# Two graph attention layers on one Trainium2 core: the first step of the pipeline in a new order

## The reference, cut to what matters

```python
# layer 0
Q, K, V = x @ W_q + b_q, x @ W_k + b_k, x @ W_v + b_v        # 8 heads of 64
a, c = x @ w_g[:D], x @ w_g[D:]                                # gates of rows and columns
scores = QK^T / 8 + a[:, :, None] + c[:, None, :] + b_g + log(adj + 1e-9)
x1 = softmax(scores) @ V + x
# layer 1
scores = where(adj == 0, -1e18, (x1 @ Wq + bq) @ (x1 @ Wk + bk)^T / sqrt(512))
x2 = x1 + (softmax(scores), 0 where adj == 0) @ x1 @ Wc
out = layernorm(x2) * gamma + beta
```

## Time and profile before

| what | value |
|---|---|
| median of 3 runs | 2256.19 us (2255.06 to 2257.74) |
| the profiled execution: its own time | 2256.57 us |
| its span in the profile | 2254.7 us |
| PE busy | 2238.5 us, 99% of the span |
| DVE, ACT, POOL busy | 1794.6, 1223.6, 987.0 us |
| TensorE clock granted, mean | 0.997 of full |

### The profile page before, as it was taken

How to read it: one execution, slowest core, us unless ns; L and a number is a source line. 1 busy time by engine, 2 the same in 40 slices (tenths; PEclk the granted TensorE clock), 3 DMA queues, 4 the chain that set the end, 5 groups by cost and what they waited for, 6 DMA issues and landing times.

```text
span 2254.7 us, 39435 instructions
## 1 busy us (share of the span) xinstructions
PE 2238.5 (99%) x13258; PEld 1866.8 (83%) x13258; DVE 1794.6 (80%) x5363; ACT 1223.6 (54%) x3489; POOL 987.0 (44%) x1139
## 2 busy tenths in 40 slices
PE   9999999999999999999999999999999999999998
PEld 6788888888888888888888888888888888888886
DVE  6778788778788787887787887878887878878775
ACT  5555555555455555555554565555555545655553
POOL 0244354553445543545434455435454344554343
PEclk9999999999999999999999999999999999999999
DMA  7333333433344333333333433333343334333321
GB/s 244 113 123 117 118 126 127 131 109 127 112 137 127 123 116 123 122 126 129 106 131 110 139 127 122 117 117 128 120 132 109 131 110 139 127 119 121 117 94 57
DMA packets 189659, 277.46 MB, mean 123 GB/s; under 512 B 24593, under 2 KB 126097, under 8 KB 185233
## 3 DMA queue, kind: packets, MB, share of 16 engines
q1 hardware_dynamic: 189168, 274.42, 37.0%
q10 hardware_dynamic: 288, 0.52, 0.1%
HBM read 166.28 MB, written 108.59 MB: 122 GB/s over the span
## 4 chain that ended last, share of the span: by engine, by line
PE 94%; DMA 2%; DVE 2%; SPq 1%; ACT 0%; issue 0%; POOL 0%; DVEq 0%; POOLq 0%
PE bank L256 27%; PE bank L258 26%; PE bank L257 26%; PE bank L509 5%; PE bank L522 5%; PE bank L551 5%; DMA turn_dram<-turned 1%; DMA probsT<-turn_dram 1%; DVE x1n L1255 0%; DVE turned L1185 0%; DMA ident<-in_ident_in 0%; SPq L318 0%; ACT probs L863 0%; SPq L349 0%; DVE probs L1166 0%
## 5 line engine op out<-in xcount | busy, mean ns | idle before, releaser
L1547 POOL TENSOR_TENSOR probs<-probs,rcp 128x512 f32<-128x512 f32 x256 | 290.5, 1151 | 875.0 <-DVE rcp L1176 874.8
L863 ACT ACTIVATE probs<-probs,nmax 128x128 f32<-128x128 f32 x1024 | 397.5, 390 | 159.7 <-DVE nmax L1166 158.3
L1255 DVE STREAM_TRANSPOSE x1n<-x1T 32x512 f32<-32x512 f32 x496 | 348.6, 703 | 38.3 <-DMA out<-x1n 30.8
L1555 POOL TENSOR_TENSOR x_lo<-xT_land,x_hi 128x512 fp32r<-128x512 f32 x124 | 168.9, 1392 | 328.0 <-ACT x_hi L809 328.0
L847 ACT ACTIVATE k_sb<-bank,cols 128x512 f32<-128x512 f32 x128 | 88.2, 689 | 270.8 <-PE bank L551 168.0
L1166 DVE CUSTOM_DVE_ANT_0 probs<-bank,bias 128x128 f32<-128x128 f32 x1024 | 227.2, 286 | 2.8
L256 PE MATMUL bank<-wc_hi,x_hi 128*128 128x512 f32 x512 | 204.3, 399 | 0.0
L256 PE MATMUL bank<-wv_hi,x_hi 128*128 128x512 f32 x512 | 203.2, 397 | 0.6 <-ACT q_sb L852 0.6
L256 PE MATMUL bank<-x_hi,wq_hi 128*128 128x512 f32 x512 | 201.9, 394 | 0.0
L256 PE MATMUL bank<-x_hi,wk_hi 128*128 128x512 f32 x512 | 199.9, 391 | 0.2
L1192 DVE SCALAR_TENSOR_TENSOR x1T<-bank,cols,xT_land 128x512 f32<-128x512 f32 x124 | 93.0, 750 | 134.2 <-PE bank L522 126.8
(11 more groups left out here) (171 smaller groups left out, 5287.3 us busy)
## 6 DMA issues: line engine op xcount, KB each, us to landing
turn_dram<-turned SPq DMA_DIRECT2D x128, 512.0 KB, 2.6
probsT<-turn_dram SPq DMA_DIRECT2D x512, 128.0 KB, 2.7
xn<-in_x SPq DMA_DIRECT2D x126, 256.0 KB, 3.2
xT_land<-in_xT SPq DMA_DIRECT2D x31, 1024.0 KB, 7.4
out<-x1n SPq DMA_DIRECT2D x124, 256.0 KB, 2.0
adj_sb<-in_adj SPq DMA_DIRECT2D x32, 256.0 KB, 3.2
c_rows<-c_dram SPq DMA_DIRECT2D x32, 256.0 KB, 3.2
at_dram<-scratch SPq DMA_DIRECT2D x30, 256.0 KB, 2.0
```

Of the source, the lines that this page charges most:

```text
L863: op = nc.scalar.activation(probs[:, k, :], probs[:, k, :], ACT.Exp, bias=nmax[:, k:k + 1], scale=-1.0, accum_out=sums[:, k:k + 1])
L1255: op = nc.vector.transpose(x1n[b * BLK:(b + 1) * BLK, :, :] .rearrange("p g (c a s) -> p a c g s", c=C, a=P // BLK)[:, a, :, :, :], x1T[a ...
L1547: nc.gpsimd.tensor_tensor(probs[:, half, :], probs[:, half, :], rcp[:, half].unsqueeze(2).to_broadcast([P, HALF, P]), ALU.mult)\
L1555: nc.gpsimd.tensor_tensor(x_lo[:, c, :], xT_land[(t + 1) % 2][:, c, :], x_hi[:, c, :].bitcast(f32), ALU.subtract).then_inc(s["pool_x"], 1)
```

## The change

Only step 0 and its neighbourhood are edited; the order of steps 1 to 31 stays as it is.

- **Gate rows.** For step 0 the trip of c through DRAM is gone. DVE multiplies the identity by c's four columns (four 128x128 products into `c_rows`), and PE multiplies a matrix of ones with it into bank 3 (`spread_first_c`, one fp32 matmul of 512 columns, between scores 1 and v of graph 2). `bias(0)` reads bank 3.
- **Loads.** The identity and the four row blocks of x are issued ahead of the column chunks 2 and 3 of Wk and Wq. Wk lands in `x1T` and no longer in `v_sb`. `gamma_b` is loaded late, with `beta_b`, behind the c spread of step 1, since `col_sum` now lies in it; `row_sum` lies in `c_rows`.
- **M.** Chunks 0 and 1 stay where they were; k and q of pairs 2 and 3 come next, then the row term and the columns; chunks 2 and 3 go behind scores 3, the last of the step.
- **DVE.** The low parts of columns 2 and 3 go behind the gates. The row sum goes behind `maxima(0, 0)`, the column sum behind `turn(0, 1)`, gates 0 and 1 of step 1 behind the low part of Wc, gates 2 and 3 of step 1 to the end of the step.
- **ACT** follows: the high parts of columns 2 and 3 behind v 1, those of M's chunks 2 and 3 behind the exponentials of pair 2.
- **SP.** Pairs 0 and 1 of step 0 are moved ahead of the loads of x's rows 2 and 3 for step 1; the c spread of step 1 goes behind the move of pair 2.

The diff by its changed lines; new semaphores' waits that only rename (`s_beta` to `s_gb`, `v_sb` to `wk_land`) are cut.

```diff
-row_sum, col_sum = (probsT[1][:, 2 * i:2 * i + 2, :, :].rearrange("p a k s -> p (a k s)") for i in (0, 1))
+row_sum, col_sum = c_rows[:, :], gamma_b[:, :]
+wk_land = x1T
...
+s_diag = sem("dve_c_diagonal")
+s_spread = sem("pe_c_spread")
...
-        if t == 0 and c == 1:
-            sp.wait_ge(s_m, C + 2)
...
-        sp.wait_ge(s_cst0, 16 * (t + 1))
-        if t > 0:
-            sp.wait_ge(s["dve_b"], nth("dve_b", t - 1))
+        sp.wait_ge(s_cst0, 16 * t)
+        if t == 1:
+            sp.wait_ge(s_m, 3)
+        sp.wait_ge(s["dve_b"], nth("dve_b", t - 1))
...
-    load_columns(v_sb, wk, "k", 0)
+    load_columns(wk_land, wk, "k", 0)
...
-    load_columns(v_sb, wk, "k", 1)
+    load_columns(wk_land, wk, "k", 1)
...
-    for c in range(2, C):
-        load_columns(v_sb, wk, "k", c)
-        load_columns(xT_land[1], wq, "q", c)
...
+    sp.dma_start(ident[:, :], ident_in).then_inc(s_const, 16)
...
-    sp.dma_start(ident[:, :], ident_in).then_inc(s_const, 16)
...
+    for c in range(2, C):
+        load_columns(wk_land, wk, "k", c)
+        load_columns(xT_land[1], wq, "q", c)
...
-    sp.dma_start(gamma_b[:, :], gamma.to_broadcast([P, D])).then_inc(s_rows, 16)
...
         else:
-            spread_c(0)
+            sp.wait_ge(s_lo["k"], C)
...
+        if not it.l1:
+            move_probs(t, 0)
+            move_probs(t, 1)
...
-        move_probs(t, 0)
-        move_probs(t, 1)
-        if it.l1:
+            move_probs(t, 0)
+            move_probs(t, 1)
...
-        spread_c(t + 1)
+            spread_c(t + 1)
...
         if not it.l1:
-            sp.wait_ge(s_m, C + 1)
-            sp.dma_start(beta_b[:, :], beta.to_broadcast([P, D])).then_inc(s_beta, 16)
+            spread_c(t + 1)
+            sp.wait_ge(s_m, 4)
+            sp.dma_start(gamma_b[:, :], gamma.to_broadcast([P, D])).then_inc(s_gb, 16)
+            sp.wait_ge(s_m, C + 2)
+            sp.dma_start(beta_b[:, :], beta.to_broadcast([P, D])).then_inc(s_gb, 16)
...
-        elif d >= 2:
-            pe.wait_ge(s["act_v"], nth("act_v", 0, d))
+        elif d == 1:
+            pe.wait_ge(s["dve_b"], nth("dve_b", 0))
+        elif d == 2:
+            pe.wait_ge(s["act_k"], nth("act_k", 0, 3))
+        else:
+            pe.wait_ge(s["act_q"], nth("act_q", 0, 3))
...
+    def spread_first_c():
+        pe.wait_ge(s_diag, 1)
+        pe.wait_ge(s["act_q"], nth("act_q", 0, 1))
+        nc.tensor.matmul(bank[3][:, :], one_c.to_broadcast([P, P]), c_rows[:, :],
+                         start=True, stop=True).then_inc(s_spread, 1)
...
         else:
-            pe.wait_ge(s["act_k"], nth("act_k", 0, 3))
+            pe.wait_ge(s_lo["m"], 3)
...
         else:
-            pe.wait_ge(s["act_q"], nth("act_q", 0, 3))
+            pe.wait_ge(s_lo["m"], 4)
...
+        spread_first_c()
...
-        for d in range(C):
-            m_chunk(d)
+        m_chunk(0)
+        m_chunk(1)
+        pe.wait_ge(s_lo["m"], 1)
+        project_k(0, 2)
+        pe.wait_ge(s_lo["m"], 2)
+        project_q(0, 2)
+        pe.wait_ge(s["act_v"], nth("act_v", 0, 2))
+        project_k(0, 3)
+        pe.wait_ge(s["act_v"], nth("act_v", 0, 3))
+        project_q(0, 3)
...
-        for c in range(2, 4):
-            pe.wait_ge(s_lo["m"], 2 * c - 3)
-            project_k(0, c)
-            pe.wait_ge(s_lo["m"], 2 * c - 2)
-            project_q(0, c)
...
+        m_chunk(2)
+        m_chunk(3)
...
     def m_high(d):
-        act.wait_ge(s_m, d + 1)
+        act.wait_ge(s_m, d + 1 if d < 2 else d + 3)
...
+        q_out(0, 1)
+        log_adj(0, 1, 0)
+        v_out(0, 0)
+        v_out(0, 1)
...
-        q_out(0, 1)
-        log_adj(0, 1, 0)
-        act.wait_ge(s_lo["k"], C)
-        v_out(0, 0)
-        v_out(0, 1)
...
-        v_out(0, 3)
...
+        v_out(0, 3)
...
-        m_high(2)
...
-        m_high(3)
...
-        for c in range(2, 4):
-            exps(0, c, 0)
-            exps(0, c, 1)
+        exps(0, 2, 0)
+        exps(0, 2, 1)
+        m_high(2)
+        m_high(3)
+        exps(0, 3, 0)
+        exps(0, 3, 1)
...
-    for c in range(2, C):
-        wk_low(c)
-        wq_low(c)
...
-        dve.wait_ge(s_crow, 16 * (t + 1))
+        if t == 0:
+            dve.wait_ge(s_spread, 1)
+            c_row = bank[3][:, :].rearrange("p (g j) -> p g j", g=GG)
+        else:
+            dve.wait_ge(s_crow, 16 * t)
+            c_row = c_rows[:, :].rearrange("p (j g) -> p g j", g=GG)
...
-        c_row = c_rows[:, :].rearrange("p (j g) -> p g j", g=GG)
...
-            dve.wait_ge(s_cst0, 16 * t)
+            if t > 1:
+                dve.wait_ge(s_cst0, 16 * (t - 1))
...
-    dve.wait_ge(s_const1, 16 * 2)
-    dve.wait_ge(s_wld1["q1"], 16 * C)
-    dve.wait_ge(s_wld1["k1"], 16)
+    dve.wait_ge(s["dve_a"], nth("dve_a", 0, 3))
+    for g in range(GG):
+        diag = nc.vector.tensor_scalar(c_rows[:, g * P:(g + 1) * P], ident[:, :], c_c[:, g:g + 1], None,
+                                       ALU.mult)
+    diag.then_inc(s_diag, 1)
+    for c in range(2, C):
+        wk_low(c)
+        wq_low(c)
...
-    weigh(row_sum, wq1_land, bk1_c, 0)
-    weigh(col_sum, [x1n[:, c, :] for c in range(C)], bq1_c, 1)
-    nc.vector.tensor_tensor(nmax1, bq1_c, bk1_c, ALU.mult).then_inc(s_sum, 1)
-    dve.wait_ge(s_rows, 16 * (C + 1))
+    def weigh_rows():
+        dve.wait_ge(s_const1, 16 * 2)
+        dve.wait_ge(s_wld1["q1"], 16 * C)
+        dve.wait_ge(s_spread, 1)
+        weigh(row_sum, wq1_land, bk1_c, 0)
+    def weigh_columns():
+        dve.wait_ge(s_wld1["k1"], 16)
+        weigh(col_sum, [x1n[:, c, :] for c in range(C)], bq1_c, 1)
+        nc.vector.tensor_tensor(nmax1, bq1_c, bk1_c, ALU.mult).then_inc(s_sum, 1)
...
-        next_gate(1, 0)
-        next_gate(1, 1)
+        weigh_rows()
...
+        m_low(0)
...
-        m_low(0)
...
-        m_low(2)
+        weigh_columns()
...
-        m_low(3)
-        dve.wait_ge(s_m, C + 1)
+        next_gate(1, 0)
+        next_gate(1, 1)
+        dve.wait_ge(s_m, 3)
...
-        dve.wait_ge(s_m, C + 2)
+        dve.wait_ge(s_m, 4)
...
-        next_gate(1, 2)
-        next_gate(1, 3)
+        dve.wait_ge(s_rows, 16 * C)
...
+        m_low(2)
...
+        m_low(3)
...
+        next_gate(1, 2)
+        next_gate(1, 3)
...
-    pool.wait_ge(s_rows, 16 * (C + 1))
...
     def affine(v, g):
+        if v == 0 and g == 0:
+            pool.wait_ge(s_gb, 16 * 2)
...
-        if v == 0 and g == 0:
-            pool.wait_ge(s_beta, 16)
...
```

More of the change, by code:

```diff
@@ L168, in gnn_program @@
         s_rows = sem("rows_loaded")
-        s_beta = sem("beta_loaded")
+        s_gb = sem("gamma_beta_loaded")
         s_hi = {n: sem(f"act_w{n}_hi") for n in "qkvmc"}
@@ L820, in wk_high @@
                 act.wait_ge(s_wld["k"][c], 16)
-                nc.scalar.activation(w_hi["k"][:, :, cols_c], v_sb[:, :, cols_c], ACT.Copy).then_inc(s_hi["k"], 1)
+                nc.scalar.activation(w_hi["k"][:, :, cols_c], wk_land[:, :, cols_c], ACT.Copy).then_inc(s_hi["k"], 1)
             def wq_high(c):
@@ L1109, in wk_low @@
                 dve.wait_ge(s_hi["k"], c + 1)
-                nc.vector.tensor_tensor(w_lo["k"][:, :, cols_c], v_sb[:, :, cols_c],
+                nc.vector.tensor_tensor(w_lo["k"][:, :, cols_c], wk_land[:, :, cols_c],
                                         w_hi["k"][:, :, cols_c].bitcast(f32), ALU.subtract).then_inc(s_lo["k"], 1)
```

## The result

The changed kernel takes 2259.97 us (median of 22 executions, 2258.52 to 2261.79), the kernel before on the same chip 2256.55 us (22 executions, 2254.02 to 2259.41): a ratio of 1.0015, 95% interval 1.0009 to 1.0022. It is slower by 3.4 us where 4.5 us less was forecast, and it lies outside the range. Its profiled execution took 2260.0 us, with a span of 2258.2 us. In this kernel `gate` is on lines 1235 and 1238, the diagonal on 1254, `bias` on 1174, the turn on 1209, `spread_first_c` on 485, the split products on 259 to 261, `m_chunk` on 459, `scores` on 526 and `pv` on 539.

A forecast was written before the change was run, and what follows sets the result against it. PE, busy for 99% of the span, bounds the kernel. With new stalls of 1.8 and 1.1 us and the clock held, 4.3 us plus small gaps give 4.5 us: 2251.7 us from the median, range 2249.8 to 2255.0.

The forecast's parts named there:

- The bound: PE busy for 99% of the span; only its waits and slow clock around step 0 can be won, about 8 us.
- PE waits nowhere else: In steps 1 to 31, order kept: no other PE waits, so the 4.5 us gain stays to the end.
- Gates and the product: Step 0's start: gates near 20.0 us, diagonal 0.9 us, product with ones adding 0.95 us on PE.
- Rival E: Late diagonal ahead of v 2 holds up PE; slower kernel, 2258.6 us if ready at 32; chance 0.05.
- The first new stall: PE before q of pair 2 waits 1.8 us for the low part of M's chunk 1, until 45.3 us.
- rival D: Clock falls in one of the two new stalls, costing up to 3.4 us: 2255.1 us; chance 0.12.
- To the last chunk and up to pv 3: PE from q of pair 2: scores 2 at 58.3 us, chunks end at 67.1, pv 2 at 83.7.
- Pair 3's move: SP's store issued near 78.6 us, 7.35 us from store to pv 3 at 85.8; PE stall 1.1 us.
- rival B: Five loads slow pair 3's store, or DVE's last gates come late: pv 3 near 88, 2253.9 us; chance 0.20.
- The clock: PE's granted clock stays at 1.00 from 40 to 95 us; pv 3 to v 2 of step 1 takes 3.15 us.
- pair 3's block at 88 and a fallen clock: At pv 3 of step 0, needed for no change in time; counted within rival B and rival D.
- The sum: v 2 of step 1 at 88.95 us against 93.28, 4.3 us sooner; with small gaps a gain of 4.5 us.

The follow-up runs named there:

- Experiment 9: Changed kernel with pair 3's store first, k of pair 3 ahead of q of pair 2, step 1's gates 0 and 1 behind pair 2's maxima: 2252.86 us, 0.9983.
- experiment 1: Changed kernel with gamma's and beta's loads moved behind pair 3's move: 2258.18 us, ratio 1.0007 to the kernel before.
- experiment 2: Changed kernel with the two loads of x's rows for step 2 moved behind pair 3's move: 2257.51 us, ratio 1.0003.
- experiment 5: Changed kernel with gamma and beta loaded late and two plain, unused loads of x's rows in their old places: 2260.16 us, ratio 1.0018.
- experiment 3: Changed kernel with pair 3's store directly behind the store of c, ahead of c_rows, x, gamma and beta: 2253.64 us, ratio 0.9987.
- experiment 12: The kernel before, unchanged, run again for a second profile: 2256.92 us against 2258.71 us for the same kernel beside it, ratio 0.9994.
- experiment 4: Changed kernel with k of pair 3 ahead of q of pair 2 on PE: 2263.07 us, ratio 1.0028.
- experiment 11: experiment 4 with POOL's first subtractions for step 1 held until v1, u1 and r0 are done: 2258.13 us, ratio 1.0009.
- experiment 6: Changed kernel with pair 3's store of step 0 issued from ACT's queue once the pair is turned: 2257.72 us, ratio 1.0005.
- experiment 8: Changed kernel with the edits of experiment 3 and experiment 4 together: 2257.22 us, ratio 1.0002.
- experiment 10: Experiment 9 with two loads of x's rows for step 2 ahead of pair 3's loads from DRAM: 2253.37 us, ratio 0.9985.

## Why the prediction was wrong, step by step

**The bound** was read rightly as to what the change can win: PE's waits and low clock in step 0's neighbourhood. Experiment 9 takes most of the 8 us against the first profile (a shift of −6.5 us) and less against the second (4.6 us) or by the medians (3.5 us). "PE waits nowhere else" was not right: the view behind the earlier trace rows also has 1.4 us at the start and 0.7 and 0.4 us in the last steps, and 0.4 us of its 5.2 us are a wait near the end, which grew to 0.8 us. A small misreading without effect: the low clock of the earlier trace rows ends at 92.8, not 92.6.

**Gates and the product**: right, with the gates 2 us early. Gates at 17.95 (forecast 20.0), a diagonal of 0.88 us (0.9) that is done by 24.5, so that the product at 26.69 had no wait. From the start of scores 1 to the end of v 2's first matmul it added 0.9 us (0.95). Rival E didn't come up. Bias at 28.38 (29.0), turn 0 at 38.00 (38.5).

**The first new stall**: right in place, cause and size, 1.86 us by `wm_lo` at 44.75 (1.8 at 45.3). That the clock holds through it was true in the profile and is not always true: rival D, which the prediction gave 0.12, occurs in two of the six profiles with this stall.

**To the last chunk and up to pv 3**: right, some 1.4 us early. Scores 2 at 56.91 (58.3), k of step 1 at 65.46, pv 2 at 82.30 (83.7).

**Pair 3's move: the step that failed.** The queue was forecast well: store of c issued at 73.64 (73.8), c_rows 76.13 (76.4), pair 3's store 78.47 (78.6). The term behind it failed: "from store to pv the trace has 80.69 to 88.04 = 7.35 us". It took 78.47 to 89.94 = 11.47 us, 4.1 more, of which 4.2 are the store itself (6.86 against 2.62 us). The loads behind it took as long as before. The prediction had worked out the price of the five loads (4.9 us of transfers) and set it aside as rival B, because the row of 2.62 us had "two loads of x and beta shortly ahead of it". SyncE's timeline of the kernel before shows that they were not under way in the same sense:

```profile
76.48 0.43 SPq L432 DMA_DIRECT2D beta_b<-in_beta  x1
76.95 0.91 SPq L303 DMA_DIRECT2D xn<-in_x  x2
80.69 0.33 SPq L314 DMA_DIRECT2D turn_dram<-turned  x1
```

They had left 3.3 to 4.2 us ahead of the store and took 4.0 to 4.3 us, so they had landed or did so within 1.1 us of its issue. In the changed kernel five had left 0.5 to 2.3 us ahead, they took 3.5 to 6.1 us, and the last of them landed 5.6 us after the store's issue. In experiments 1 and 2 three loads stand right ahead, as many as in that row, and the store takes 6.3 and 5.6 us. B had the right mechanism but was too small: it had the store landed at 83.3 and pv 3 near 88, where the profile has 85.33 and 89.94. Experiments 1, 2 and 5 show the loads issued right ahead as the cause, whichever they are, and experiment 3 removes the stall by the order alone.

**The clock** was the second error, and it hangs on the first. The forecast stall of 1.1 us lies between one of 0.63 us, at 79.55, behind which the clock stayed at 1.00 until 86 us, and those of 1.9 us, behind which it fell in two of six profiles; with 6.55 us it was at 0.50: pv 3 to v 2 took 89.94 to 95.35 = 5.41 us, 2.3 more than the 3.15 of the forecast. Together: 88.95 + 4.14 + 2.26 = 95.35, the row. The prediction had named this pair ("pair 3's block at 88 and a fallen clock") and given it no chance of its own, and it came 1.9 us later still.

**The sum.** Forecast −4.3 us at v 2 of step 1, measured +2.07: 6.4 us, by the two terms above. The medians differ from the forecast by 7.9 us (3.4 + 4.5). The remaining 1.5 us arise later: the shift of the changed kernel grows from 2.1 us in step 4 to 2.6 in step 24 and 3.5 us at the span's end, of which 0.8 us are longer waits for turned blocks at 2127 and 2191 (experiment 12); why they grew is open. The fall of the clock at q of pair 2 has no part in this, since the profiled execution, whose own time is the median, didn't have it. "The shift stays to the end" was true to within −0.2 to 2.3 us, which is as much as such a change is worth.

## What to carry to other kernels

A transfer's duration belongs to what is in flight with it: before a row's duration is used in a new place, look up which transfers are still under way when it is issued, there and in the row, and not only which stand ahead of it in the queue (the same store took 2.6 us behind three loads that had all but landed and 5.6 to 6.3 us right behind three), and put the transfer on which the busiest engine waits ahead of those that have slack. When a gap on the bound engine is closed by a new order, look up which engine pairs then lie beside each other; experiment 4 lost more by that than its gap was worth. Where the whole effect is a few us out of 2250, take two profiles of the kernel before: up to v 2 of step 1 its own two differ by 1.8 us, and its medians by up to 2.3 us.

## What the runs showed of the hardware

**DVE and POOL hold each other up.** A gate pass (two inputs in SBUF) beside POOL's subtraction (also reading SBUF) took 1.76 us instead of 0.69, and four subtractions 6.67 us instead of 4.96. Each of POOL's four took 1.65 to 1.72 us instead of 1.27, so both engines lost. The Trainium skill, page "SBUF — State Buffer", section "Who interferes with whom", states that a DVE instruction with two SBUF inputs contends with a GpSimd instruction that reads SBUF. These rows agree, and experiment 11 shows it by keeping the two apart; which of the two is held at a time, and for how long, they don't show.

**The same stall doesn't always have the same price.** The 1.9 us wait of PE at 43 to 45 us left the clock at 1.00 in four profiles and let it fall to 0.50 for 3.4 us in two. In the kernel before, the wait ahead of pv 3 (4.46 and 3.90 us) had 6.8 us of low clock in one execution and 3.4 in another.

**A store from another engine's queue** beside loads of SyncE's took 5.5 us (experiment 6); with nothing but the 2 KB store of c ahead it took 3.2 to 3.8 us (experiments 3, 8, 9 and 10). A second queue didn't take it past the traffic here.
